# Attention with a two-stage LayerNorm end: three chunks of the end work moved from the last head group into groups five to seven, through the score banks

## The reference, cut to what matters

```
Q, K, V = heads of x @ Wq.T, x @ Wk.T, x @ Wv.T
O       = causal softmax(Q K.T / 4) V            (per head, float32)
x       = layernorm(x + O @ Wo.T)
l       = max(|x|, 1e-12) / 127 per token;  r = the same per column of rhs
x       = layernorm(x + (int8(x / l) @ int8(rhs / r)) * l * r)
```

## Time and profile before

| | us |
|---|---|
| median of 3 runs | 1012.61 (1010.09 to 1015.05) |
| the profiled execution, its time | 1015.52 |
| its span, first to last instruction | 1013.8 |
| busy: PE / DVE / ACT / POOL | 946.2 / 821.1 / 710.9 / 264.3 |

### The profile page before, as it was taken

How to read it: one execution, slowest core, us unless ns; L and a number is a source line. 1 busy time by engine, 2 the same in 40 slices (tenths; PEclk the granted TensorE clock), 3 DMA queues, 4 the chain that set the end, 5 groups by cost and what they waited for, 6 DMA issues and landing times.

```text
span 1013.8 us, 34409 instructions
## 1 busy us (share of the span) xinstructions
PE 946.2 (93%) x14884; PEld 474.4 (47%) x14884; DVE 821.1 (81%) x1083; ACT 710.9 (70%) x1470; POOL 264.3 (26%) x431
## 2 busy tenths in 40 slices
PE   8899999999999999999999999999999999999862
PEld 5555545544554454445444644454444444434331
DVE  5488878887888788878887888788878886799797
ACT  3434348787878877887888788878877687777630
POOL 4443442102210221022102210211022104456534
PEclk9999989999999999999999999999999999999985
DMA  5556530001210121022002200220022050434501
GB/s 176 163 180 183 153 116 10 8 9 45 69 36 9 49 66 34 9 58 64 28 8 66 64 24 6 72 65 19 8 72 68 11 132 14 131 84 115 147 32 52
DMA packets 71836, 67.29 MB, mean 66 GB/s; under 512 B 15113, under 2 KB 65609, under 8 KB 71685
## 3 DMA queue, kind: packets, MB, share of 16 engines
q1 hardware_dynamic: 71684, 65.10, 22.9%
HBM read 43.25 MB, written 21.35 MB: 64 GB/s over the span
## 4 chain that ended last, share of the span: by engine, by line
PE 71%; DVE 14%; ACT 7%; DMA 3%; issue 2%; POOL 1%; SPq 1%; POOLq 0%; DVEq 0%; ACTq 0%
PE ps_acc L723 20%; PE ps_max L679 19%; PE ps_score L679 18%; DVE block_max L970 6%; ACT PR L922 6%; PE ps_score L602 4%; PE ps_score L609 2%; PE ps_max L677 2%; PE ps_max L697 2%; DVE stats L1084 1%; DMA end_slots<-heads_out 1%; ACT accS L910 1%; DMA V<-heads_out 1%; PE ps_max L797 1%; DVE end_slots L1094 1%
## 5 line engine op out<-in xcount | busy, mean ns | idle before, releaser
L970 DVE TENSOR_REDUCE block_max<-ps_max 128x2 f32<-128x1024 f32 (+3 forms) x640 | 653.8, 1061 | 141.8 <-PE ps_max L679 68.6
L922 ACT ACTIVATE PR<-ps_score 128x512 f32<-128x512 f32 (+3 forms) x1280 | 620.3, 539 | 169.0 <-PE ps_score L679 150.0
L679 PE MATMUL ps_score<-QS,KS 99*32 99x512 bf16 (+3 forms) x5120 | 418.0, 351 | 22.7 <-ACT PR L922 19.2
L679 PE MATMUL ps_max<-KS,QS 96*32 96x512 bf16 (+3 forms) x4544 | 329.2, 350 | 7.4 <-DVE block_max L970 5.3
L723 PE MATMUL ps_acc<-PR,VG 128*32 128x512 f32 (+3 forms) x2560 | 299.1, 534 | 0.0
L679 PEld LDWEIGHTS ps_score<-QS,KS 99*32 99x32 bf16 x5120 | 150.3, 96 | 216.9 <-ACT PR L922 119.3
L679 PEld LDWEIGHTS ps_max<-KS,QS 96*32 96x32 bf16 x4544 | 126.3, 97 | 141.8 <-DVE block_max L970 59.8
L1192 POOL TENSOR_SCALAR_AFFINE_SELECT PR<-PR 128x512 f32<-128x512 f32 x128 | 81.6, 638 | 285.8 <-ACT PR L922 285.8
L697 PE MATMUL ps_max<-mask_q,ident_b 128*32 128x64 bf16 (+3 forms) x1808 | 96.1, 200 | 0.0
L723 PEld LDWEIGHTS ps_acc<-PR,VG 128*32 128x32 f32 x2560 | 79.3, 110 | 35.4 <-issue 3.5
L1200 POOL CAST max_parts<-neg_max 16x128 bf16<-16x128 f32 (+1 forms) x30 | 8.7, 289 | 224.9 <-ACT neg_max L905 223.5
(11 more groups left out here) (126 smaller groups left out, 525.0 us busy)
## 6 DMA issues: line engine op xcount, KB each, us to landing
QS<-qparts SPq DMA_DIRECT2D x192, 64.0 KB, 2.4
KS<-kparts SPq DMA_DIRECT2D x192, 64.0 KB, 2.4
qparts<-end_slots SPq DMA_DIRECT2D x16, 384.0 KB, 3.8
kparts<-end_slots SPq DMA_DIRECT2D x16, 384.0 KB, 3.1
PR<-in_L_attn_x SPq DMA_DIRECT2D x8, 512.0 KB, 4.4
heads_out<-accS SPq DMA_DIRECT2D x124, 32.0 KB
end_slots<-in_L_attn_x SPq DMA_DIRECT2D x4, 512.0 KB, 9.4
out_y<-end_slots SPq DMA_DIRECT2D x8, 256.0 KB, 2.1
```

Of the source, the lines that this page charges most:

```text
L679: m = pe.matmul(bank[t * QW:t * QW + QW, 0:w], stack[:, t * QW:t * QW + QW], moving, start=True, stop=stop)
L922: act.activation(PR[:, k % 4, j, 0:w], ps_score[:, score_slot(pos), 0:w], ACT.Exp, scale=SCALE).then_inc(s_exp, 1)
L970: dve.tensor_reduce(block_max[:, h * PAIR:h * PAIR + PAIR, i, b], ps_max[:, slot_at:slot_at + PAIR, 0:w], AX.X, ALU.max).then_inc(s_reduce ...
```

## The change

The six halves of the first three chunks of batch 0 are placed in the fifth, sixth and seventh group, one chunk in each: projections from step 12, 8 and 4 of the group, second halves 18 steps later. They don't use `ps_max`: each projected tile, turned half and product takes a bank of the score ring in its turn, ACT takes it out (copy to SBUF for tiles and turned halves; for the product a multiplication with the row's scale), DVE adds the projection from SBUF, and POOL multiplies the product with the weights' scales. `quota` runs for each group and knows the costs of these parts. Sums are brought 8 steps before a chunk's start, sent back 6 before, loads 4 before, outputs 2 before; DVE inverts each chunk's sums by itself behind the items of its step. The chunks use four slots. The fourth chunk of batch 0 and the four of batch 1 stay in the last group, with starts at its steps 2, 5, 14, 17, 22, 25, 34, 36 and behind its end. Projection and product, in the last group too, are written as four matmuls side by side on 32 columns of weights each (`tiled`) in place of one on 128. The queue of SP issues the end work's DMAs in every group behind what it had at that step.

The diff, cut to its core (in order: constants and due steps, the planner, SP's group and its end parts, PE's group and its soon parts with `tiled`, DVE's group, POOL's second residual):

```
+    ENDS = B * CHUNKS
+    SOON = 3
+    SOON_HALVES = 2 * SOON
+    SLOT = [0, 1, 0, 1, 2, 3, 0, 1]
+    SLOTS = 4
+    ALL = GROUPS * NS
+    FIRST_END, LAST_GROUP = 4 * NS, (GROUPS - 1) * NS
+    SOON_START = [FIRST_END + 12 + 36 * m for m in range(SOON)]
+    CHUNK_START = SOON_START + [LAST_GROUP + k for k in (1, 14, 22, 34, 35)]
+    PROJECT_START = [at + 2 * s for at in SOON_START for s in range(2)]
+    HALF_START = [at + 18 * s for at in SOON_START for s in range(2)] + \
+        [LAST_GROUP + k for k in (2, 5, 14, 17, 22, 25, 34, 36)] + [ALL + 1, ALL + 2]
+    CHUNK_DUE = dict(sums_in=-8, sums_back=-6, load=-4, outputs=-2)
+    SOON_DUE = dict(residual=5, rstd1=6, norm1=7, quantise=8, to_int=9, turn=10, product=12, residual2=13, moments2=14,
+                    rstd2=15, norm2=16, store=17)
+    DUE = dict(project0=0, project1=0, residual=1, rstd1=2, norm1=3, quantise=3, to_int=5, turn=6, take=6, product=7,
+               scale=8, residual2=9, moments2=10, rstd2=11, norm2=12, store=13)
...
+    PE_END = dict(project0=2048, project1=2048, product=1024, turn=800)
+    DVE_END = dict(residual=4600, norm1=2000, quantise=6000, moments2=2900, norm2=2000)
...
-                if k % BATCH == BATCH - 1:
-                    at += sum(HG * (CH - skip(*STEPS[k - back])) for back in range(LAG, LAG + BATCH))
+                at += work(k, PE_END) + HG * (CH - skip(*STEPS[k - LAG]))
+                done = max(done, at if work(k, DVE_END) else 0) + work(k, DVE_END)
...
+                        if k in STACKS_AT and 0 < g < GROUPS - 1:
+                            load_stacks(nq, np_, STACKS_AT.index(k))
+                        end_parts(NS * g + k)
+
+                def end_parts(k):
+                    for m in chunks_due(k, "sums_in"):
+                        sums_in(m)
+                    for m in chunks_due(k, "sums_back"):
+                        sums_back(m)
+                    for m in chunks_due(k, "load"):
+                        load(m)
+                    for e in due(k, "store"):
+                        store_result(e)
...
+                        soon_parts(NS * g + k)
+                        end_parts(NS * g + k)
...
+                    for t in range(TPH):
+                        for e in soon_due(k, f"project{t}"):
+                            m, s = divmod(e, 2)
+                            use, at = USE[f"project{t}", e], s * HALF + t * P
+                            pe.wait_ge(e_on, HALVES * (m + 1))
+                            pe.wait_ge(s_exp, use - BANKS + 1)
+                            for h in range(HALVES):
+                                y = tiled(ps_score[:, bank_of(use), 0:D], o_in(m)[:, h, at:at + P], wT[:, 3, h, :], h)
+                            y.then_inc(s_st, 1)
+
+                def tiled(out, stack, moving, h):
+
+                    for r in range(0, P, QW):
+                        y = pe.matmul(out[r:r + QW], stack[:, r:r + QW], moving, start=h == 0, stop=h == HALVES - 1)
+                    return y
...
 (DVE: the items and the end work by steps)
+                def group(g):
+                    n = 0
+                    for k in range(NS):
+                        while n < QUOTA[g][k][-1]:
+                            on, m = STREAM[KIND[g]][n]
+                            item(g + on, m, maxima_use(g + on - 1, ITEMS[m][0] // TPC) + 1 if g + on else 0)
+                            n += 1
+                        end_parts(NS * g + k)
...
+                            pool.wait_ge(s_exp, USE["product", e] + 1)
+                            for t in range(s * TPH, s * TPH + TPH):
+                                pool.tensor_tensor(work(m)[:, t, :], work(m)[:, t, :], ffn_scale[:, :], ALU.mult)\
+                                    .then_inc(e_wide, 1)
```

More of the change, by code:

```diff
@@ L100, in build @@
     LATE = [c for c in range(CHUNKS) if LAST_ITEM[c] >= AHEAD]
+    KIND = ["steady"] * (GROUPS - 2) + ["full", "last"]
     STREAM = dict(
@@ new lines, in build, with due @@
+    CHUNK_DUE = dict(sums_in=-8, sums_back=-6, load=-4, outputs=-2)
[3 more added lines that the diff above has]
+               scale=8, residual2=9, moments2=10, rstd2=11, norm2=12, store=13)
+    DONE_AT = max(HALF_START) + max(DUE.values())
+    def due(k, part):
+        first = PROJECT_START if part in ("project0", "project1") else HALF_START
+        soon = {"project0": 0, "project1": 1, **SOON_DUE}
+        return [e for e in range(SOON_HALVES) if part in soon and first[e] + soon[part] == k] + \
+            [e for e in range(SOON_HALVES, 2 * ENDS) if part in DUE and HALF_START[e] + DUE[part] == k]
@@ L116, in quota @@
+    def quota(stream, g):
         made = lambda m: PAIR * (max(ITEM_COLS[m] // PAIR, LOAD) + (LOAD if ITEMS[m][1] == ITEMS[m][0] // TPC else 0))
         read = lambda m: READ_FROM + READ * ITEM_COLS[m]
+        work = lambda k, parts: sum(cost * len(soon_due(NS * g + k, part)) for part, cost in parts.items())
         def place(pace, early):
@@ L137, in quota, with turn_after @@
                     for out in [place(pace / 100, early)] if out) if stream else [[0] * HG for _ in STEPS]
[L139 to L149, removed]
+    QUOTA = [quota(STREAM[KIND[g]], g) for g in range(GROUPS)]
+    def turn_after(g, on, c):
+        place = STREAM[KIND[g]].index((on, LAST_ITEM[c]))
+        return min(NS - 1, min(k for k in range(NS) if QUOTA[g][k][-1] > place) + 1)
+    TURNS = [[(turn_after(g, 0, c), 0, c) for c in LATE] + [(turn_after(g, 1, c), 1, c) for c in EARLY]
+             for g in range(GROUPS - 1)] + [[(1 + n, 0, c) for n, c in enumerate(LATE)]]
+    for turns in TURNS:
         assert all(k + 3 < FIRST[c] for k, on, c in turns if not on) and turns == sorted(turns, key=lambda t: t[0])
-    STACKS_AT, FULL_LOADS = [0, 1, 8, 16], 30
+    STACKS_AT = [0, 1, 8, 16]
     XCHUNKS = B * CHUNKS
@@ L166, in build, with bank_order @@
     assert FRONT_QUOTA[-1][-1] == AHEAD
[L171 to L174, removed]
     RESTS = 3
[L176 to L198, removed]
-        return {use: n for n, use in enumerate(order)}
[L201 to L216, removed]
+    BANKS = 3
+    def bank_order():
+        order = [("first",)]
+        for g in range(GROUPS):
+            for k in range(NS):
+                order += [("score", g, k, j) for j in range(HG)]
+                for part in ("product", "turn", "project0", "project1"):
+                    order += [(part, e) for e in soon_due(NS * g + k, part)]
+                order += [("maxima", g + on, c) for at, on, c in TURNS[g] if at == k]
+        return {use: n for n, use in enumerate(order)}
+    USE = bank_order()
+    score_use = lambda g, k, j: USE["score", g, k, j]
+    maxima_use = lambda g, c: USE.get(("maxima", g, c), 0)
+    bank_of = lambda use: use % BANKS
     def item_use(g, n):
@@ L725, in values, with group @@
                     m.then_inc(s_pv, 1)
[L727 to L730 removed]
+                def group(g):
+                    q, p = divmod(g, 2)
+                    groups = [(q, p), divmod(g + 1, 2)]
                     n = 0
```

415 lines of the change are left out of this document (191 added, 224 removed).

## The result

The kernel with the change takes 1052.3 us (1046.3 to 1058.9), against 1012.8 (1010.1 to 1015.1) for the kernel before on the same chip: a ratio of 1.039, with a 95% interval from 1.032 to 1.046. The forecast was 1046, in a range from 1010 to 1066. The profiled execution took 1058.9 us, with a span of 1057.0, so 43.2 more than the span before.

The account below looks back on a forecast made before the run. PE bounds the sixth group; PE and DVE both fill the last. Terms -17.7 - 3.2 + 16.2 + 35.5 + 6.2 - 3.7 + 2 - 2 = +33.3 us on the profiled 1015.5 give 1048.8, as median 1046; range 1010 to 1066.

Parts of the forecast that it names:

- The waits for the loads: Groups five to seven and last: PE waits for POOL's outputs behind late loads, 11.0 + 9.2 + 9.6 + 5.7 = +35.5 us.
- lie ahead of these waits and vanish in them: Fifth and sixth group: DVE's waits for sums, about 3 us, add nothing because SP sets each load wait's end.
- The fourth wait: Step 2 of the last group: PE waits 5.7 us for the fourth chunk's outputs.
- The clock: After each of four load waits PE runs at a lowered clock, 1.56 us lost each, +6.2 us together.
- PE's work in the groups and DVE's: Groups five to seven: six halves at 2.7 us of PE work, +16.2 us; DVE near its bound in the seventh, +2.
- The last group: Last group: gives up six halves at 2.95 us, -17.7 us; sixteen tiled projections at 0.2 us, -3.2.
- Inversions: Seventh group: the inversions in one piece go, with PE's 2.17 us idle time and 1.56 us of clock, -3.7 us.
- tail: Behind the last group: loses remnants of halves that now end earlier, some 3 us of DVE work, -2 us.
- half of the waits: Rival: PE reaches the projections later than thought, having already lost time before them; 1029 us, chance 0.07.
- The loads are there in time: Rival: no load waits, end work moves to groups where DVE has 17 us to spare; 1004 us, chance 0.14.
- DVE's long pieces stop PE: Rival: quantising holds DVE over 2 us per piece and stops PE, 22 us more; 1068 us, chance 0.10.

Follow-up runs that it names:

- the kernel with single inversions: The kernel before, with its four inversions placed singly behind every fourth item from the middle of the seventh group: 1009.5 us, ratio 0.9962.
- the kernel with tiling: The kernel before, with inversions placed singly and projections and products as four column tiles, all still in the last group: 1009.3 us, ratio 0.9951.
- the shortened pieces: Loads 8 steps earlier than in the changed kernel, DVE's residual, statistics, normalising and quantising for six early halves on 16 of 256 columns: 1028.6 us, ratio 1.015.
- only handovers and no plan: Loads 16 steps earlier, early halves' DVE, PE, ACT and POOL work cut to 16 or 32 columns and struck from the plan placing DVE's items: 1008.8 us, ratio 0.996.

## Why the prediction was right, and where it was not

The sign and the place were right. The size came near because two errors cancelled, which was luck: for groups five to seven the forecast had 34.5 us for late loads and their clock (29.8 + 4.7) and 18.2 for all else that the halves cost there, and the runs show 21.1 and 41.5. In the profile the three groups are 62.6 us longer than in the kernel with single inversions. Taken off one after the other, in the order of the runs (another order could share it out in another way):

| taken off | groups five to seven, us | median, us |
|---|---|---|
| late loads: PE's waits and clock | 21.1 | 16.0 |
| ACT waiting for the quantised half | 3.6 | 5.3 |
| stacks late behind the loads | 6.2 | 3.5 |
| PE's and DVE's volume | 9.8 | 6.2 |
| ACT's and POOL's volume | 2.9 | 6.9 |
| the plan around the halves | 5.6 | 5.6 |
| what is left: bank handovers, turns, short pieces | 13.4 | |

- **The waits for the loads** were put at 35.5 us. The mechanism held where SP sets it: the load's first issue came 28.9, 18.7 and 5.6 us after the start of the fifth, sixth and seventh group (forecast 28.7, 18.0 and 6.3), and PE left the wait at 41.2, 29.4 and 16.9 us (41.8, 31.1 and 19.4), since the way from a load's first issue to the start of its outputs took 9.8, 8.2 and 8.7 us and not 10.5. But the length of the wait failed: 17.6 us in three, not 29.8. The step at fault is "lie ahead of these waits and vanish in them", with the wait counted from where PE stood in the kernel before. PE came to the places later than that, at 34.2 us and not 30.8 in the fifth group. There it had waited for DVE, whose inversion stood behind the sums' DMA for 1.7 us (DVE, then PE):

```profile
563.61 0.20 DVE L1075 TENSOR_SCALAR sums<-sums 128x64 f32<-128x64 f32 x1 [1.66 <-DMA sums<-row_sums]
```
```profile
565.62 0.62 PE L651 MATMUL ps_max<-KS,QS 96*32 96x512 bf16 x8 [2.05 <-DVE block_max L990]
```

  The whole delay at the three places is 10.4 + 8.4 + 7.1 = 25.9 us against the kernel before. The loads are not the cause of all of it: with them 8 steps earlier PE begins the same tiles at 34.7, 25.1 and 11.1 us, which is 16.6 us less than after and still 9.3 more than before; with them 16 steps earlier it is 5.3 more. PE would have been late there without any late load.
- **The fourth wait**, 5.7 us in the last group, was not there. Chunk 3's outputs begin at 913.40 and its first tile at 916.05, and PE shows no idle time before it: the last group's first score block was at 911.8, so this is 4.2 us in. On the forecast's clock PE stood there at 853.4 and the group's start at 849.0, which is 4.4: PE was on time, and so was the load: its first issue (904.64) was 7.2 us ahead of the group, and not 3.0 as forecast, with nothing of the stacks before it in this step.
- **The clock** was put at 1.56 us per wait, after a wait that was as short as 2.17. It held after the first (0.60 over four us), was 2.0 after the third (0.51), and 2.9 after the second, where the low stretch went on beyond the four us shown above (5.9 x 0.49):

```profile
692.60:698.50 5.90, 5.87 (x75) 2.88 (x79) 0.67 (x2) 1.62 (x4) 1.81 (x5) 0.51 0.46 132
```

  But the clock fell at two more places, after waits of PE for ACT of 1.68 and 1.30 us (618.94 and 665.85), which I had not forecast:

```profile
617.00:625.00 8.00, 6.09 (x83) 2.44 (x73) 3.52 (x6) 4.40 (x12) 1.36 (x3) 0.79 0.01 2
667.00:671.00 4.00, 4.00 (x64) 2.29 (x60) 2.40 (x2) 2.98 (x8) 1.06 (x2) 0.59 0.34 95
```

  8 x 0.21 + 4 x 0.41 = 3.3 us more: 9.8 in the three groups, and not 4.7. In the kernel with the loads earlier a wait just as long (1.68 at 610.38) went by at a clock of 1.00, while after one of 1.31 us at 809.60 it was 0.72 over six us; what decides is not settled by these runs.
- **PE's work in the groups and DVE's** were put at 16.2 + 2. This is the step that failed most. Without any late load, the six halves cost 335.8 - 304.1 = 31.7 us, or 5.3 per half and not 3.0. I had counted instructions, and the ring's handovers had no price of their own: they only put the 2.7 near the upper end of its bounds. The runs with the work taken out say that handovers, turns and what is left of the short pieces together still cost 13.4 / 6 = 2.2 us per half; how this divides among them no run shows. The wait of ACT for the quantised half and the late stacks were in no step of mine. The plan I had taken for a protection; in the seventh group it cost PE 5.0 us of idle time where only the handovers were left, and the group was 2.9 us longer with it where the work was whole.
- **The last group** was put at -17.7 - 3.2 = -20.9, or -15.2 with the wait. It was -18.3 in the profile, with no fourth wait. What is missing is the clock, and not the halves' price: PE waited twice for the outputs of other chunks, and the group ran at 0.95, not 0.99.

```profile
945.22 1.93 PE L766 MATMUL ps_max<-wT,V 128*32 128x256 f32 x16 [2.05 <-POOL V L1273]
...
1002.15 1.92 PE L766 MATMUL ps_max<-wT,end_slots 128*32 128x256 f32 x16 [2.48 <-POOL end_slots L1273]
```

  In the other kernels with moved halves this group took 100.8 and 101.3 us where the clock stayed at 1.00, and 105.1 to 106.3 where it was 0.95. Against the 123.5 of before that is up to -22.7, so the price of 2.95 us per half was not too high. These waits at the last group's other chunks were in no step of the forecast.
- **Inversions** -2.9 (forecast -3.7), **tail** -1.3 (-2).

Of the rivals, "half of the waits" came near in its mechanism, and failed in its time, because it took the delay ahead of the waits for free. "The loads are there in time" had 1004 us; that kernel, run, takes 1036, and 1027 at its best. So no faster kernel was found behind the late loads: a half costs 5.3 us in groups five to seven at the best schedule tried. It gives back (160.9 - 147.6) / 6 = 2.2 in the last group and tail of that same kernel, measured against the kernel with tiling, and at most (160.9 - 140.9) / 6 = 3.3 in any kernel run with whole halves. Of the kernels that do all their work the faster ones move nothing: single inversions in the kernel before, 0.996 of its time, and 0.995 with tiling.

"DVE's long pieces stop PE" had a chance of 0.10 and a price of 22 us. The waits are there, but smaller. PE's waits for DVE's maxima in the three groups grew from 3.5 to 11.0 us by the change, and the shortened pieces took only 1.0 of that away. DVE's quantising also holds up ACT and through it PE, for 3.6 to 5.3 us in all.

## What to carry to other kernels

Before work is moved between stages, measure what a unit of it costs at the new place with its whole chain, the handovers too, and not only its instructions: here the fullest engine of the old stage was relieved, and the new stage had one engine at 97.5 of 99.8 us. A wait that is found in a profile is worth its length only if the engine comes to that place no later without it, and if no other wait takes its place. And a queue is part of a schedule: a load that is due at a step starts when everything issued before it is through.

## What was not expected of the hardware

The same sixteen matrix products behind the last group's scores took 5.06 us in one kernel and 9.24 in another. PE had stood 1.18 us before them in the one and 2.77 in the other. PE's timeline with the loads 8 steps earlier, then with the loads 16 steps earlier and the whole numbers later, and the window over each:

```profile
993.55 5.06 PE L817 MATMUL ps_max<-wT,end_slots 128*128 128x256 f32 x16 [1.18 <-DVE end_slots L1169]
```
```profile
993.50:998.60 5.10, 5.05 (x20) 2.43 (x24) 3.76 (x12) 0.00 (x0) 1.52 (x3) 1.00 0.01 3
```
```profile
986.46 9.24 PE L817 MATMUL ps_max<-wT,end_slots 128*128 128x256 f32 x16 [2.77 <-DVE end_slots L1169]
```
```profile
986.40:995.70 9.30, 9.24 (x20) 4.06 (x24) 4.04 (x12) 0.00 (x0) 1.52 (x3) 0.50 0.01 2
```

After 1.18 us of idle time PE was granted the full clock, after 2.77 half of it, for all of the 9.3 us. The traces of all eleven kernels with moved halves agree: in seven PE had stood 0.97 to 1.23 us there and the products took 5.06 us, in four it had stood 2.63 to 2.77 and they took 9.24. No run changed this wait alone, so that it decides is argued and not shown. It took 4.2 us back from the faster kernel, whose last group and tail together last 147.6 us against 140.9. The tail of 46 to 47 us, instead of 39 to 40, appears in the same four kernels, among them the one with only handovers and no plan. It is a reason why the medians follow the groups' sums loosely.
